# Attention with sixteen heads and a routed feed-forward layer on one core: a product and two row sends placed elsewhere in the pass, a plan spread out, copies and a table load moved

## The reference

```python
x = layernorm(x + attention(x))          # no scale or shift
x = layernorm(x + experts(x))

def attention(x):                        # 16 heads of 8
    s = (Q @ K.T) / sqrt(8); s = where(causal, s, -1e6)
    return concat(softmax(s) @ V) @ Wo + bo

def experts(x):
    xn = (x - mean) / sqrt(var + 1e-5) * gamma + beta
    p = softmax(xn @ Wg.T)               # 8 experts
    (t1, e1), (t2, e2) = top two of p    # gates t1, t2 / (t1 + t2 + 1e-9)
    y_e = gelu(xn @ W1[e] + b1[e]) @ W2[e] + b2[e]
    return x + gate1 * y_e1 + gate2 * y_e2
```

## Time and profile before

| | |
|---|---|
| device time, median of 3 | 1002.54 us |
| profiled execution's own time | 1002.12 us |
| its span, first to last instruction | 1000.2 us |
| granted TensorE clock, mean | 0.972 of full |
| busy PE / PEld | 879.0 / 567.0 us |
| busy DVE / ACT / POOL | 749.2 / 676.8 / 652.2 us |
| one attention pass (L719 to L719, from 445.42) | 39.05 us |
| y and x2 of one sequence | 512 KB, 256 KB |

### The profile page before, as it was taken

How to read it: one execution, slowest core, us unless ns; L and a number is a source line. 1 busy time by engine, 2 the same in 40 slices (tenths; PEclk the granted TensorE clock), 3 DMA queues, 4 the chain that set the end, 5 groups by cost and what they waited for, 6 DMA issues and landing times.

```text
span 1000.2 us, 29035 instructions
## 1 busy us (share of the span) xinstructions
PE 879.0 (88%) x9185; PEld 567.0 (57%) x9185; DVE 749.2 (75%) x2069; ACT 676.8 (68%) x1393; POOL 652.2 (65%) x907
## 2 busy tenths in 40 slices
PE   5689899999999999989999998859999999998960
PEld 2234354444444444444444444339999989998850
DVE  1787779888888888888888888935554565469867
ACT  1377687777787777777777777735566655656753
POOL 6243555778777687786786786756767657556652
PEclk9799999999999999999999999979999999999995
DMA  7525535636436455354345332343232223266625
GB/s 200 189 72 157 171 97 157 189 101 193 146 122 204 118 158 169 101 151 159 105 157 163 98 129 58 83 129 87 78 87 87 82 80 91 77 206 208 194 79 170
DMA packets 169380, 132.51 MB, mean 132 GB/s; under 512 B 52938, under 2 KB 155377, under 8 KB 169104
## 3 DMA queue, kind: packets, MB, share of 16 engines
q1 hardware_dynamic: 156880, 112.48, 37.7%
q0 software_dynamic: 8704, 17.06, 5.1%
q10 hardware_dynamic: 3648, 1.12, 0.5%
HBM read 71.55 MB, written 61.15 MB: 133 GB/s over the span
## 4 chain that ended last, share of the span: by engine, by line
PE 40%; POOL 7%; issue 6%; DVE 5%; ACT 3%; DMA 1%; SPq 1%; ACTq 0%; POOLq 0%; DVEq 0%
PE ring L1196 13%; PE ring L1212 13%; PE ps_v L1132 4%; PE ring L1069 2%; DVE negmax L1243 2%; POOL probs L642 2%; ACT probs L772 2%; PE ring L1100 2%; PE ps_v L1186 1%; POOL rs L704 1%; PE ps_m L946 1%; DVE probs L1585 1%; PE ring L1115 1%; POOL xin L660 1%; POOL qarea L606 1%
## 5 line engine op out<-in xcount | busy, mean ns | idle before, releaser
L1243 DVE TENSOR_REDUCE negmax<-ring 128x2 f32<-128x1024 f32 (+3 forms) x512 | 408.1, 815 | 71.2 <-PE ring L1115 68.2
L772 ACT ACTIVATE probs<-ring 128x768 f32<-128x768 f32 (+1 forms) x384 | 336.1, 880 | 111.4 <-PE ring L1069 105.7
L642 POOL TENSOR_SCALAR_AFFINE_SELECT probs<-probs 128x512 f32<-128x512 f32 x256 | 163.7, 643 | 164.3 <-ACT probs L772 162.1
L890 ACT ACTIVATE vpad<-ring,b_s 128x128 f32<-128x128 f32 x576 | 165.0, 369 | 112.3 <-PE ring L1196 100.9
L688 POOL DMA_INDIRECT y_d<-vpad,xs x144 | 146.5, 1017 | 100.0 <-DVE vpad L1555 60.8
L1132 PE MATMUL ps_v<-probs,vpad 128*32 128x512 f32 (+3 forms) x2048 | 183.5, 448 | 9.9 <-POOL probs L642 9.9
L1196 PE MATMUL ring<-vpad,w_t 128*128 128x128 f32 x1152 | 156.1, 279 | 7.4 <-issue 7.2
L1212 PE MATMUL ring<-qarea,vpad 128*128 x1152 | 155.0, 277 | 2.9 <-issue 1.8
L1196 PEld LDWEIGHTS ring<-vpad,w_t 128*128 128x128 f32 x1152 | 141.7, 194 | 10.2 <-issue 9.9
L680 POOL DMA_INDIRECT rows_d<-xn,slot x128 | 127.1, 993 | 30.2 <-issue 26.3
L1212 PEld LDWEIGHTS ring<-qarea,vpad 128*128 128x128 f32 x1152 | 139.8, 191 | 6.9 <-issue 6.0
(11 more groups left out here) (187 smaller groups left out, 1168.8 us busy)
## 6 DMA issues: line engine op xcount, KB each, us to landing
kside<-qk_d SPq DMA_DIRECT2D x32, 512.0 KB, 6.0
qk_d<-qarea SPq DMA_DIRECT2D x32, 384.0 KB, 2.7
xs<-rows_d SPq DMA_DIRECT2D x144, 66.0 KB
qk_d<-qarea SPq DMA_DIRECT2D x32, 256.0 KB, 2.2
qarea<-qk_d SPq DMA_DIRECT2D x16, 512.0 KB, 6.0
qodd<-qk_d SPq DMA_DIRECT2D x16, 512.0 KB, 6.3
probs<-y_d SPq DMA_DIRECT2D x16, 512.0 KB
xin<-L_attn_x SPq DMA_DIRECT2D x16, 256.0 KB, 3.7
```

The source lines that it names most:

```text
L642: pool.affine_select(out=diag, in_=diag, pattern=[[0, 4], [1, P]], compare_op=ALU.is_ge, fill=0.0, base=0, channel_multiplier=-1).then_inc ...
L772: nc.scalar.activation(of_unit(h // 2, part), ring[:, 2 * part % 3, :, (0, P, P)[part]:S], ACT.Exp, scale=SCALE).then_inc(sem("exp_done"), 1)
L890: ins = nc.scalar.activation(ht[:, n % 4, c, :], ps_a[:, n % 4, c * P:(c + 1) * P], ACT.Gelu_apprx_tanh, bias=b1_s[:, bass.ds(e, 1), c:c + ...
L1243: ins = nc.vector.tensor_reduce(negmax[:, n // 6 % 2, qb, s:s + 2], ring[:, (2 * n + 1) % 3, :, c0:c0 + nk], AX.X, ALU.max, negate=True)
```

## The change

- GpSimd's product with gamma goes from h = 6 to h = 5. Row sends 0 and 1 of a sequence go out at h = 11 and h = 13 of the pass before, and the other six at h = 0 to 3, so that none is left at h = 5.
- The first part of `divide` goes from half step 29 to 30 (reciprocal) and 31 (product).
- In pass 15 `rstd` goes behind the last mask. `copy_u` at h = 4 goes behind the exponential, in pass 16 to h = 1.
- A gelu of one column at h = 3 of pass 16 has no use but to bring its function table in.
- `first_tiles` turns tile 0 ahead of the wait for the weights, and VectorE loads the expert numbers and copies the first weights ahead of its waits.
- The second plan's ten parts lie at half steps 14, 16, ..., 30 and 31.
- From tile 104 on ScalarE copies the turned rows, behind the gelus of tile n.
- The x2 loads of sequences 12 to 15 are issued three tiles apart, from tile 135 on, ahead of the y loads.

```diff
-                    if rb.exists(NB) and h in (6, 8, 9):
-                        make_rows(pool, rb, (6, 8, 9).index(h))
+                    if rb.exists(NB) and h in (5, 8, 9):
+                        make_rows(pool, rb, (5, 8, 9).index(h))
+                    if h in SEND_SOON and i.value < NB:
+                        send_rows(late, SEND_SOON[h])
...
-                    if prev.exists(NB) and h == 14:
+                    if prev.exists(NB) and h == (15 if i.value == NB - 1 else 14):
...
-            SEND_IN = {0: (0,), 1: (1,), 2: (2, 3), 3: (4, 5), 5: (6, 7)}
+            SEND_SOON = {11: 0, 13: 1}
+            SEND_IN = {0: (2,), 1: (3,), 2: (4, 5), 3: (6, 7)}
...
-                    if h == 4 and prev.exists(NB):
-                        copy_u(act, prev, 1)
+                        if h == (1 if i.value == NB else 4) and u == 0 and prev.exists(NB):
+                            copy_u(act, prev, 1)
...
+                if h == 3 and i.value == NB:
+                    nc.scalar.activation(warm[:, :], tiny[:, :], ACT.Gelu_apprx_tanh)
...
+            def turned(n):
+                act.wait_ge(sem("tile_turned"), n + 1)
+                act.wait_ge(sem("h_ready"), n - 3)
+                nc.scalar.activation(xst[:, n % 4, :], turn_bank(n)[:, 0:P], ACT.Copy).then_inc(sem("xst_late"), 1)
             for n in STEPS:
                 hidden(n)
+                if TILE0[1] <= n + 2 < NT:
+                    turned(n + 2)
...
-                        if i.exists(NB) and at == 29:
-                            divide(i, 0, False)
-                            divide(i, 0, True)
+                        if i.exists(NB) and at in (30, 31):
+                            divide(i, 0, at == 31)
...
-                        if not i.loop and i.value == NB + 2 and 16 <= at < 18 + E:
-                            if at == 16:
+                        if not i.loop and i.value == NB + 2 and (at in range(14, 32, 2) or at == 31):
+                            if at == 14:
                                 last_segment()
-                            plan_part(1, at - 16)
+                            plan_part(1, (at - 13) // 2)
...
             def first_tiles():            # VectorE
+                dve.wait_ge(sem("experts_in"), 16 * (2 * E + 1))
+                for n in (0, 1):
+                    experts[n] = expert_of(n)
+                weights(0)
                 dve.wait_ge(sem("pv_done"), 4 * NB)
-                dve.wait_ge(sem("experts_in"), 16 * (2 * E + 1))
+                turned(0)
                 dve.wait_ge(sem("b1_turned"), 1)
...
+            def load_x2(b):
+                if b == FIRST[1]:
+                    sp.wait_ge(sem("x2_stored"), 16 * NB)
+                if b >= 4:
+                    sp.wait_ge(sem("z_done"), b - 3)
                 sp.dma_start(x2_t[:, b % 4], x2_d[b]).then_inc(sem(f"y_in{b % 4}"), 16)
...
+                b = last_stage(n, 3)
+                if b is not None and FIRST[1] <= b + 4 < NB:
+                    load_x2(b + 4)
```

More of the change, by code:

```diff
@@ L1171, in first_tiles @@
                 pe.wait_ge(sem("u_copied"), 2 * NB)
+                turn_tile(0)
                 pe.wait_ge(sem("experts_in"), 16 * (2 * E + 1))
@@ L1519, in first_tiles @@
                     sem("b1_ready"), 1)
-                for n in (0, 1):
-                    experts[n] = expert_of(n)
-                weights(0)
-                turned(0)
                 turned(1)
```

18 lines of the change are left out of this document (13 added, 5 removed).

## The result

The changed kernel takes 999.9 us (median of 20 runs, 994.5 to 1004.2) against 1003.1 us of the kernel before (20 runs, 1000.0 to 1006.2): 0.9966 of it, 95% interval 0.9953 to 0.998. That is 3.2 us less, where 7.8 had been forecast. A second comparison gave 0.9972 (0.9957 to 0.9988), 2.7 us less. Its profiled execution took 1000.98 us, span 999.0 us, granted clock 0.975. Ratios leave out single runs that were slower as a whole, such as one of gamma_fourth that took 1417.2 us at a granted clock of 0.559.

The account below looks back on a forecast made before the run. TensorE was taken as the bound, its small idle times in the passes to be won and full in the expert tiles. Terms -6.8 + 0 + 0 - 0.5 + 1.5 - 1.2 - 0.8 = -7.8 gave 994.7 us; range 989.5 to 1000.2.

Parts of the forecast that it names:

- Product with gamma, -6.8 forecast: Attention passes: moved to h = 5, it no longer stretches VectorE's cast at h = 8, shortening ten passes; -6.8 us.
- rival 1: Attention passes: the stall moves to the row addition, the product's term is -1.5 instead of -6.8; 1000.0 us, chance 0.15.
- Division: End of each attention pass: reciprocal and product only change places with the last two maxima; 0, at best -5.9 us.
- Row sends: Attention passes: two sends at h = 11 and 13 fit into GpSimd's waits; their small cost is within the -6.8 us.
- rival 4: Attention passes: the moved sends hold VectorE in its full stretch, making the kernel slower; 1007 us, chance 0.05.
- Turn to the experts, -0.5 forecast: Before the first expert tile: its DMA still decides, only the gelu table load moves to idle time; -0.5 us.
- Plan, +1.5 forecast: Second plan beside the expert tiles: each spread part pays by itself where every second was free; +1.5 us.
- the upper end of 2.2: Second plan: the forecast's worst case for spreading its parts, given as 8 x 0.57; +2.2 us.
- Rival 3: Second plan: spreading its parts is a gain, -2.6 us instead of +1.5; 990.6 us, chance 0.18.
- Turned copies, -1.2 forecast: Tiles from 104 on: with the copies on ScalarE, the next tile's weights come 0.2 us sooner; -1.2 us.
- x2 loads, -0.8 forecast: Last four batches: with x2 loaded earlier VectorE waits for 512 KB of y alone; -0.8 us.
- the end of -1.45: Last four batches: the forecast's largest gain from the earlier x2 loads, a third of 4.34 us; -1.45 us.

Follow-up runs that it names:

- gamma_fourth: Kernel before with only the product with gamma at h = 5 and two row sends moved to h = 11 and 13; 0.9977 of the kernel before.
- divide_back: Changed kernel with reciprocal and division back at half step 29; 1000.64 us, 0.9975 of the kernel before.
- mask_between: Changed kernel, plan in successive half steps, gates product behind half step 14's maximum, mask 15 between rstd's sixth and seventh steps; 0.9913 of the kernel before.
- gates_later: Changed kernel with the gates product behind the maximum of half step 14 instead of 12; 0.9888 of the kernel before (1060 us there).
- plan_back: Changed kernel with the second plan's parts back in successive half steps 16 to 25; 0.9903 of the kernel before (1060 us there).
- turned_back: Changed kernel with the second segment's turned tiles copied by VectorE again; 0.9921 of the kernel before (1060 us there).
- start_back: Changed kernel with the last pass and the turn to the experts as before; 1003.73 us, 0.9998 of the kernel before.

## Why the prediction was right or wrong

**Product with gamma, -6.8 forecast: wrong.** The step of the prediction that failed is the sentence that the product then lies "among maxima and a reciprocal that read PSUM". The gates product, with two operands in SBUF, stands right there, 0.13 us ahead of it in the passes where all is on time (480.14, 480.27) and behind it in the others. Where it is ahead, the step was right but for its size: 38.35 us a pass instead of 38.2, since 0.13 us of the shorter wait come back by the query product and the mask of head 15 takes 0.08 (0.35 in gamma_fourth and divide_back against 0.27 before). Where it is behind, half a microsecond is lost, in four of the ten passes of the kernel after. That is rival 1 with another instruction: the row addition took 0.98 us in every good pass (486.48) and nobody waited for it, as the forecast said. That the measured 999.9 is the time of rival 1, 1000.0, is luck: it took another instruction, and other terms that missed. What the forecast left out altogether is pass 15, where the collision came in every execution with the gates product in its place on the chip of 1003 us: TensorE waits 0.46 to 0.92 us for the maximum behind it. gamma_fourth shows 3.6 us lost between pass 14 and tile 4 and 5.2 gained before; of the 3.6, these 0.9 are read as the collision's and the rest is not placed. Measured with the sends: 2.3 us, and 4.8 at the edge of the interval, so less than the 6.8.

**Division: right.** 0 forecast, 1000.64 against 1000.86 measured. The reason was half right: the waits merged as expected (0.39 and 0.42 into 0.62 and 0.21), but the wait for the mask behind the factors grew from 0.35 to 0.55 us, which the forecast did not have, and mask_between shows mask and factors both on the path.

**Row sends: right as far as seen.** No run moves them alone. The passes with the two sends at h = 11 and 13 are 38.35 us, which the waits named above account for; rival 4 has no trace. The one-hot beside a send is still lengthened in places, as before: L1360 took 0.53 us at 515.14 beside the send of 514.64 and ended with it. The Trainium skill ("SBUF — State Buffer", section "SBUF: two separate sides") says that the instruction that starts first keeps the shared ports; the two gates products, of 0.18 and 0.89 us, agree with it; the 1.67 us of gamma_fourth (last section) is not explained by it. What the prediction took from it as a rival, that the sends cost as much, did not show here.

**Turn to the experts, -0.5 forecast: right in its mechanism, short in its size.** No table load before the first gelu, first tile still with its DMA; the part as a whole measured 2.9 us by time, some 1.5 either way, and which of its edits gives that is open.

**Plan, +1.5 forecast: right in sign, too small.** It cost 2.5 us. The argument held to the row: waits 4.36 us apart, nine instead of five. The term was sized at 0.5 us for each of eight pairs less 2.6. Nine waits from 807.66 to 843.1 are eight distances of 35.4 us together against 30.3 (8 x 3.79), 5.1 us, where before four distances cost 2.6. That is 2.5. The mis-sized term is the 0.5 us a pair, where most pairs took the 0.57 that its own rows had and one took 1.02 (a distance of 4.81). The 2.5 is above the upper end of 2.2 too, which is itself summed wrong: 8 x 0.57 less 2.6 is 2.0. Rival 3 is excluded.

**Turned copies, -1.2 forecast: wrong.** The step that failed is that the weights of the next tile, coming 0.2 us sooner, would be what TensorE waits for. The copy that left VectorE is late on ScalarE instead (releaser L940 at 950.93), 0.65 became 0.61, and the idle time ahead of the first products stayed at 6.1 us against 6.2.

**x2 loads, -0.8 forecast: right in its mechanism, short in its size.** 3.41 us from the first y issue to the first addition against 4.76, -1.35, inside the end of -1.45. The stage is 1.7 us shorter in the first pair of profiles; over all of them it is 37.8 to 38.1 us with the loads moved and 39.1 to 39.6 without, 1.4 on average. No run undoes this part alone.

The sum with what was measured: -2.3 (product and sends, turn included) - 2.9 - 1.4 + 2.5 + 0 to 0.8 for the copies, between -4.1 and -3.3, beside a measured -3.2 and -2.7. The intervals of the parts (2.5 us each way for the first, 1.5 for the second) are wider than the difference, so the sum agrees but proves no single term.

## What to carry to other kernels

When an instruction is moved away from a collision, list everything that VectorE runs in its new slot with both operands in SBUF, however small, and how far each is from its start: here an instruction 0.13 us ahead was untouched and one 0.40 us behind lost over half a microsecond. Look at the irregular last pass by itself, since there the order is different and something large may hang on it. And moving work out of a full engine gives nothing where the receiver's copy then arrives as late as the one it replaced. Last, a variant of the full change needs the full change beside it in the same group of runs: gates_later, plan_back and turned_back had only the kernel before beside them, on a chip where all kernels took longer, and their times could not be read against the kernel after.

## What was not expected of the hardware

A product of 128x4 numbers on VectorE, 0.15 us by itself, took 1.67 us in pass 15 of gamma_fourth: it did not run when GpSimd's product ended (627.44) but held on to the end of the mask that followed it without a gap (627.39 + 0.64 = 628.03). start_back has the same, 1.69 us, to the end of the mask. In pass 15 of the kernel after the gates product ended with the product with gamma, and the copy of 0.15 us behind it (L1509) took 0.65, to the end of the mask. So back-to-back GpSimd instructions can cost more than the first of them; in pass 5 the mask followed without a gap too, and nothing behind the gates product was held. What decides it isn't shown. And one and the same program took 1003 us in two groups of runs on one chip and 1060 in three groups on three others, with the attention passes nearly alike (427.9 and 432.1 us) and the tiles fed by row transfers 19% longer (133.2 and 158.7).
